# The third layer's expert products as four matmuls of 32 stationary columns each

## The reference

```python
router_logits = x @ gate_weight.T                 # x: 1024 tokens x 256; 8 experts
probs = jax.nn.softmax(router_logits, axis=-1)
top_v, top_i = jax.lax.top_k(probs, 2)            # two experts for each token
top_v = top_v / top_v.sum(axis=-1, keepdims=True)
combine_w = einsum('tke,tk->te', one_hot(top_i, 8), top_v)

def expert_step(acc, inp):
    gu, dp, w = inp                               # gu: 1024 x 256, dp: 256 x 512
    gate, up = jnp.split(x @ gu.T, 2, axis=-1)    # 512 columns each
    hidden = jax.nn.silu(gate) * up
    y = hidden @ dp.T
    return (acc + w[:, None] * y, None)
```

## Time and profile before

| | us |
|---|---|
| runs | 458.54, 454.34, 457.25 |
| median | 457.25 |
| span of the profiled execution | 455.4 |
| TensorE busy, all of the span | 407.7 |
| stretch of the expert blocks | about 249 to 395 |
| granted TensorE clock, mean of the span | 0.970 |

### The profile page before, as it was taken

How to read it: one execution, slowest core, us unless ns; L and a number is a source line. 1 busy time by engine, 2 the same in 40 slices (tenths; PEclk the granted TensorE clock), 3 DMA queues, 4 the chain that set the end, 5 groups by cost and what they waited for, 6 DMA issues and landing times.

```text
span 455.4 us, 6054 instructions
## 1 busy us (share of the span) xinstructions
PE 407.7 (90%) x1749; PEld 265.4 (58%) x1749; DVE 328.5 (72%) x620; ACT 239.2 (53%) x478; POOL 253.2 (56%) x352
## 2 busy tenths in 40 slices
PE   7798999999899989957967999999999999976895
PEld 7576787555455545535753455566655566653554
DVE  5998789999999999799874466557546311038994
ACT  6533682667667667579853233232333232339883
POOL 5474037676879996137506457856864553214641
PEclk9999999999999999989965999999999999999998
DMA  7900006456555645000115987898898885050011
GB/s 230 411 11 0 1 1 221 138 185 224 184 158 191 212 163 184 1 1 2 39 55 178 376 299 280 304 374 299 305 361 300 285 317 192 35 184 1 23 35 37
DMA packets 23665, 77.39 MB, mean 170 GB/s; under 512 B 3441, under 2 KB 7921, under 8 KB 20177
## 3 DMA queue, kind: packets, MB, share of 16 engines
q1 hardware_dynamic: 20336, 69.94, 43.5%
q0 software_dynamic: 2208, 6.03, 4.1%
q10 hardware_dynamic: 1088, 1.05, 0.7%
HBM read 71.76 MB, written 5.24 MB: 169 GB/s over the span
## 4 chain that ended last, share of the span: by engine, by line
PE 50%; DVE 28%; issue 12%; ACT 3%; POOL 3%; DMA 3%; SPq 0%; DVEq 0%; POOLq 0%; ACTq 0%
PE bank L1993 18%; PE bank L2013 10%; PE bank L1770 5%; DVE hx L1295 4%; DVE fw L1084 4%; DVE bw L1087 3%; PE bank L1615 3%; PE bank L1617 2%; PE bank L1616 2%; DVE fw L1092 2%; PE bank L2004 2%; DVE xp L1353 2%; PE bank L1692 2%; DVE gl L1574 2%; PE bank L1839 1%
## 5 line engine op out<-in xcount | busy, mean ns | idle before, releaser
L1993 PE MATMUL bank<-gu,xbT 128*128 128x512 f32 x184 | 84.6, 603 | 0.9 <-ACT xbT L920 0.9
L1770 PE MATMUL bank<-hx,w2raw 128*128 128x512 f32 x128 | 67.3, 607 | 4.6 <-DVE hx L1295 3.7
L1510 DVE TENSOR_TENSOR hm<-bank,sl 128x512 f32<-128x512 f32 x23 | 15.9, 692 | 69.3 <-PE bank L1993 37.9
L808 ACT ACTIVATE rl<-bank 128x512 f32<-128x512 f32 x64 | 38.1, 595 | 38.6 <-PE bank L1617 37.8
L1993 PEld LDWEIGHTS bank<-gu,xbT 128*128 128x128 f32 x184 | 35.2, 194 | 36.3 <-issue 33.8
L1615 PE MATMUL bank<-xlhi,w1hi 128*128 128x512 f32 x64 | 49.4, 771 | 0.0
L2013 PE MATMUL bank<-dn,hT 128*128 128x256 f32 x184 | 45.2, 389 | 3.4 <-ACT hT L931 0.8
L589 POOL DMA_INDIRECT y_rows<-yb,dest_i x23 | 25.0, 1088 | 35.4 <-ACT yb L937 34.8
L1295 DVE TENSOR_TENSOR hx<-bank,cwb 128x512 f32<-128x512 f32 x64 | 42.1, 660 | 3.1 <-ACT bank L812 3.1
L2013 PEld LDWEIGHTS bank<-dn,hT 128*128 128x128 f32 x184 | 33.1, 190 | 11.8 <-issue 8.2
L1092 DVE RECIPROCAL fw<-fw 128x256 f32<-128x256 f32 x23 | 39.8, 1732 | 0.0
(11 more groups left out here) (305 smaller groups left out, 931.7 us busy)
## 6 DMA issues: line engine op xcount, KB each, us to landing
gu<-in_gu SPq DMA_DIRECT2D x22, 1024.0 KB, 7.6
cwb<-cw_rows SPq DMA_DIRECT2D x32, 512.0 KB, 4.1
dn<-in_dn SPq DMA_DIRECT2D x23, 512.0 KB, 4.5
traw<-in_t SPq DMA_DIRECT2D x3, 1024.0 KB, 7.5
w1raw<-in_w SPq DMA_DIRECT2D x8, 256.0 KB, 4.9
w2raw<-in_w SPq DMA_DIRECT2D x8, 256.0 KB, 4.6
kT<-in_kt SPq DMA_DIRECT2D x4, 256.0 KB, 4.5
x<-in_x SPq DMA_DIRECT2D x2, 512.0 KB, 6.4
```

The lines of the kernel that those rows point to most:

```text
L808: act.activation(rl[:, u % 3, :], bank[u % 4][:], ACT.Relu).then_inc(sem("r_ready"), 1)
L1770: pe.matmul(bank[4 + s][:], w2raw[:, e // 4 % 2, e % 4, :], hx[:, 0, u % 4, :], start=(e == 0), stop=(e == E0 - 1), skip_group_check=True) ...
L1993: ins = pe.matmul(bank[2 * (b % 2) + up][:], xbT[:, b % 2, k, :], gu[:, b % RING, k, up * I2:up * I2 + I2], start=(k == 0), stop=(k == KC ...
```

## The change

Each matmul call of `gate_up` and `block_down` becomes four. Call `s` takes the stationary columns of tokens `32 s` to `32 s + 31` and writes the same 32 partitions of the bank; the moving operand is the whole one each time. The chunk loop stays outside, the four quarters inside. The semaphore's increment stays on the last call of the group. The transposes, the transfers and all other engines' instructions are as before.

```diff
+PART = 32
@@ gate_up
                     for k in range(KC):
-                        ins = pe.matmul(bank[2 * (b % 2) + up][:], xbT[:, b % 2, k, :], gu[:, b % RING, k, up * I2:up * I2 + I2],
-                                        start=(k == 0), stop=(k == KC - 1))
+                        for s in range(P // PART):
+                            own = slice(s * PART, s * PART + PART)
+                            ins = pe.matmul(bank[2 * (b % 2) + up][own, :], xbT[:, b % 2, k, own],
+                                            gu[:, b % RING, k, up * I2:up * I2 + I2], start=(k == 0), stop=(k == KC - 1))
                     ins.then_inc(sem("up_done" if up else "gate_done"), 1)
@@ block_down
-                    ins = pe.matmul(y_bank(b), hT2[:, b % 2, j, :], dn[:, b % RING, j, :], start=(j == 0), stop=(j == 3))
+                    for s in range(P // PART):
+                        own = slice(s * PART, s * PART + PART)
+                        ins = pe.matmul(y_bank(b)[own, :], hT2[:, b % 2, j, own], dn[:, b % RING, j, :], start=(j == 0), stop=(j == 3))
                 ins.then_inc(sem("d_done"), 1)
```

## The result

The changed kernel takes 458.94 us in the median of 20 runs (457.40 to 462.97), the kernel before 457.14 (454.34 to 459.69): ratio 1.0056, 95% interval 1.0037 to 1.0075, or 1.7 to 3.4 us more. The forecast was 590 with a range from 570 to 828. It was wrong: rival B, all four quarters abreast, is what happened, with a small new cost beside it.

A forecast was written before the change was run, and what follows sets the result against it. The prediction took TensorE to bound the expert blocks; overlap of only two records added 133.2 us to the profiled span of 455.4, and with 1.85 for the runs' median gave 590 us, range 570 to 828.

The forecast's parts named there:

- rival B: In the expert products all four quarters stream abreast: 455.5 us, or 464 with the issue limit; chance 0.12.
- What bounds the kernel: In the third layer's expert blocks TensorE binds; added work arrives nearly one to one; its waits total 1.7 us.
- The price of a narrow record, and the count: Expert-block quarter records save no array time, 0.4285 or 0.2155 us each; in turn +355.6 us; TensorE count 2853.
- The order of the records: Expert-block records start in program order, so only two overlap at hand-overs: 17 slots a product, +133.2 us.
- Changing the width: Four steps a block between 32-column matmuls and full-width transposes cost 0; other end 15.1 us in all.
- Issue rate: 64 pairs a block, 65 ns each, are hidden; with four abreast, 8.2 us more in `block_down`.
- What is given back: First `block_down` load shrinks, at most 1.7 us; waits may go; first block stays about 5.18 us; all set at 0.
- The sum: Profiled span 455.4 + 133.2 = 588.6 us; with the runs' median 1.85 above the span, 590.4, said as 590.

The follow-up runs named there:

- experiment 1: Changed kernel with all calls writing partitions 0 to 31, so all on one column quarter, leaving out most tokens' results: 814.24 us, one run.
- experiment 8: Kernel before, full width, with the hidden transposes moved between the gate and up products: 453.83 us, ratio 0.9925.
- experiment 2: Changed kernel with quarters as the outer loop and chunks inside, in each product: 527.43 us, ratio 1.1539.
- experiment 5: Changed kernel with four records in a row for each quarter, in both products: 461.36 us, ratio 1.0109.
- experiment 6: Changed kernel with six records in a row for each quarter, in the down product alone: 496.48 us, ratio 1.0906.
- experiment 4: Changed kernel with the down product's moving operand split in two halves of 128 columns, 64 pairs a block there: 460.00 us, ratio 1.0062.
- experiment 9: Changed kernel with only gate and up quartered and the old full-width call of `block_down`: 462.82 us, ratio 1.0146.
- experiment 12: Changed kernel with hidden transposes between gate and up, and next block's gate and up weights issued ahead of down weights: 460.82 us, ratio 1.0099.
- experiment 3: Changed kernel with halves, two calls of 64 stationary columns, in place of quarters: 459.91 us, ratio 1.0073.
- experiment 7: Changed kernel with the up product full width again, gate and down still quartered: 461.28 us, ratio 1.0115.

## Why the prediction was wrong

*What bounds the kernel*: right. TensorE bounds the blocks; what is added to it arrives one to one (experiment 1: +357 measured, +355.6 worked out). But the 1.7 us of waits from the earlier trace rows are not all that it stands still: in each block it waits 0.3 us for ScalarE's copy of the hidden values (the last transpose starts at 284.00 + 0.11 and holds the array for 0.11, the down product starts at 284.51), and the rows of waits miss more than half of it, since the transpose's record runs on into it (to 284.38). Experiment 8 took it out of the period.

*The price of a narrow record, and the count*: right. 0.4285 us on the same quarter, 2853 records.

*The order of the records*: this is the step that failed. "Starts on TensorE are in program order throughout these rows" was true of rows that all use the whole array and so can't overlap; I carried it over to quarters, where it decides. From it followed that the next call's first record can start only after the second record of the call before, 17 slots in place of 8, and +133 us of which nothing came: gate and up take 3.58 us, not 7.28, and down 1.72, not 3.66. In experiment 2 records of a later product start ahead of those of an earlier one, and experiments 2, 5 and 6 together fit what there is instead: an order within each quarter, with room for three waiting records.
The Trainium skill ("TensorE: Matmul & The Clock Gate", Part 3, What overlaps and what doesn't) has the overlap of column groups right (3.43 us against 13.7), but its strict order of all matmuls is not what these runs show: experiment 2 has starts out of program order.

I had named this mechanism as rival B with its place and its price, and gave it 0.12. The evidence against it that I put down, "no row has a matmul starting ahead of an earlier one", was the same empty evidence. That the 458.94 us lie between B's 455.5 and 464 is in part luck: of its terms only the saved open load came, the issue limit did not, and the changes of width, which it lacks, did.

*Changing the width*: taken as 0 on the strength of the earlier trace rows; it is 0.09 us at each step that other work doesn't hide, plus 0.05 for the last quarter's later start, plus the load that is no longer pulled ahead (0.055 ahead of transposes, 0.105 ahead of a 128-column product). I also counted four steps in a block. There are two, one into the transposes and one out of them, since the down product and the next gate product are both quartered; so the bound was 23 x 2 x 0.164 = 7.5 us, not 15.1. One step into the transposes, 0.20 in all, is more than its 0.164. The row misled: the first layer's step from `128*32` to `128*128` loses nothing (49.05 to 49.29), the blocks' steps do, and what tells the two apart is not shown by any run. The use of several quarters is not it: experiment 1, with quarter 0 alone, shows the open load as well (299.81, its last record ended at 285.98 + 13.90 - 0.592 + 0.4285 = 299.72).
The Trainium skill ("TensorEngine Tiling (Array Packing)", Key Properties) says that changing the tiling mode drains the engine. In the blocks the runs agree, with 0.09 us a change; the first layer's step shows none.

*Issue rate*: 65 ns a pair was no floor. 27 ns a pair were sustained (experiment 4), and a pair has 54 ns in the down product and twice that in gate and up, so neither is near a limit.

*What is given back*: the 0.08 us ahead of the down product came as foreseen (1.80 to 1.72). The first block's products took 3.64 us in place of 5.18, on a granted clock of 1.00 in 249 to 255 us where it was 0.73. That is not put down to the change: in the same stretch the quartered kernels of experiments 4, 5, 9 and 12 have 0.72, 0.75, 0.79 and 0.72, those of 3 and 7 have 1.00.

*The sum*, with what was measured: -0.08, +0.15, +0.05 a block, 22 times +0.12 is 2.6 us, and the three one-column sums add 3 x 0.26 = 0.8. The ratio's 0.56% of 457 is 2.6, with an interval from 1.7 to 3.4; so 3.4 lies at its end, and the traces, which lose and regain 1 us outside the blocks, don't settle the rest.

## What to carry to other kernels

Splitting the stationary columns of a full-width product over the array's quarters gains nothing: the moving operand streams four times, side by side, and takes as long as once. What four quarters do save is seen against experiment 1: 32 records of 32 columns take 13.7 us on one quarter and 3.43 on four. Such calls should change quarter at least every four records, without changes of width between them. When a row is to prove a rule of order, ask whether the instructions in it could have broken it; and when an engine is the bound, look first at its short regular pauses and at what is queued behind a wait, which here gave 1.7%.

## What the runs showed of the hardware that I had not expected

- Column quarters and halves run abreast for f32 products too, with two records to a call: 4 x 0.4285 us of work in 0.43 (experiment 1 and the changed kernel).
- Each quarter takes its records in its own order; as far as these orders test it, one runs, three wait, and a full line stops what is behind it (527.43 us with eight in a row, 496.48 with six, 461.36 with four).
- A step between the blocks' 32-column products and 128-column ones opens 0.09 us in either direction (experiments 7 and 9), one from 64 to 128 as much (experiment 3), and no load is pulled ahead across it. The first layer's step is an exception that stays unexplained.
- 27 ns for a pair of load and matmul was sustained over 64 pairs (experiment 4).
- A pause of 2.5 us in the blocks was followed by a stretch on a granted clock of 0.56, which cost 1.65 us more (experiment 8).
